# Linear attention taken as (q·k)·v instead of q·(k·v), with whole heads for GpSimd and inverse deviations by exp and ln

## The reference

```python
xn = _ln(q_x, ln1_w, ln1_b)
q, k, v = (heads of xn @ wq + bq, xn @ wk + bk, xn @ wv + bv)   # 16 heads of 16
fq = jax.nn.elu(q) + 1.0
fk = jax.nn.elu(k) + 1.0
kv = jnp.einsum('bhnd,bhne->bnde', fk, v)      # summed over the heads of a token
qkv = jnp.einsum('bhnd,bnde->bhne', fq, kv)
k_sum = fk.sum(axis=1)
qk = jnp.einsum('bhnd,bnd->bhn', fq, k_sum)
attn = qkv / (qk[..., None] + 1e-06)
x = q_x + attn @ wo + bo
x = x + gelu(_ln(x, ln2_w, ln2_b) @ fc_w + fc_b) @ proj_w + proj_b
```

## Time and profile before

| what | value |
|---|---|
| median of 3 runs | 1926.57 us (1924.77 to 1927.19) |
| the profiled execution, its own time | 1925.68 us |
| its span in the profile | 1924.0 us |
| PE, DVE, ACT, POOL busy | 1741.5, 1277.6, 806.8, 1269.4 us |
| mean granted clock of PE | 0.931 |
| chain that ended last | PE 83%, POOL 5%, ACT 5%, DVE 3% |

### The profile page before, as it was taken

The page is one execution under the profiler, slowest core; times in us unless marked ns, Lnnn a source line. Parts: engine busy times, 40 slices in busy tenths (PEclk is TensorE's granted clock), DMA queues, the critical chain, the costliest instruction groups (busy, mean ns, idle before and its releaser), DMA issues.

```text
span 1924.0 us, 26018 instructions
## 1 busy us (share of the span) xinstructions
PE 1741.5 (91%) x7160; PEld 1248.5 (65%) x7161; DVE 1277.6 (66%) x2339; ACT 806.8 (42%) x1547; POOL 1269.4 (66%) x749
## 2 busy tenths in 40 slices
PE   3489998898999989989999899887999999999997
PEld 1255565555655655556556555555888888888886
DVE  7988898988988989889889898713222222222221
ACT  2245455464454554644545546332332333333232
POOL 5876888888988888789888888812333333333333
PEclk8698898998988988989889889888999999999999
DMA  5101110101101101011011010005766666666664
GB/s 187 41 14 44 45 44 22 44 30 36 34 20 44 44 22 44 31 35 44 11 44 44 22 44 24 27 28 171 163 159 157 157 161 162 162 164 159 157 156 91
DMA packets 87130, 148.57 MB, mean 77 GB/s; under 512 B 8640, under 2 KB 71872, under 8 KB 86720
## 3 DMA queue, kind: packets, MB, share of 16 engines
q1 hardware_dynamic: 60512, 112.58, 18.3%
q0 software_dynamic: 26592, 35.67, 11.0%
HBM read 101.79 MB, written 48.56 MB: 78 GB/s over the span
## 4 chain that ended last, share of the span: by engine, by line
PE 83%; POOL 5%; ACT 5%; DVE 3%; issue 2%; DMA 1%; SPq 0%; POOLq 0%; ACTq 0%; DVEq 0%
PE p_b L1210 17%; PE p_b L1258 11%; PE p_b L1289 10%; PE p_b L1350 9%; PE p_b L1361 9%; PE p_q L1350 7%; PE p_q L1182 5%; PE p_v L1350 3%; PE p_b L1281 3%; PE p_v L1182 3%; PE p_b L1196 2%; POOL prod_pool L461 2%; PE p_xT L1337 2%; ACT bT L628 1%; ACT L639 1%
## 5 line engine op out<-in xcount | busy, mean ns | idle before, releaser
L574 POOL DMA_INDIRECT out_rows<-prod_pool,prod x142 | 220.7, 1554 | 384.3 <-ACT prod_pool L742 353.9
L461 POOL TENSOR_TENSOR prod_pool<-prod_pool 128x544 f32<-128x544 f32 (+4 forms) x240 | 399.6, 1665 | 18.8
L1258 PE MATMUL p_b<-bT,fc_sb 128*128 128x512 f32 x512 | 226.5, 601 | 12.1 <-ACT bT L671 12.1
L1210 PE MATMUL p_b<-proj_sb,hid 128*128 128x256 f32 x1024 | 230.5, 379 | 0.0
L834 DVE TENSOR_REDUCE kvT<-prod 128x128 f32<-128x2048 f32 x96 | 219.4, 2286 | 2.7
L826 DVE TENSOR_TENSOR prod<-p_q,v_dve 128x4096 f32<-128x4096 f32 x48 | 211.9, 4414 | 0.0
L1289 PE MATMUL p_b<-bT,sgup_sb 128*128 128x512 f32 x384 | 208.1, 700 | 0.0
L1210 PEld LDWEIGHTS p_b<-proj_sb,hid 128*128 128x128 f32 x1024 | 189.6, 190 | 27.7 <-issue 0.5
L1350 PE MATMUL p_b<-prod,exp_up 128*128 128x256 f32 x840 | 187.1, 379 | 0.0
L1258 PEld LDWEIGHTS p_b<-bT,fc_sb 128*128 128x128 f32 x512 | 96.8, 192 | 132.4 <-issue 108.6
L864 DVE TENSOR_REDUCE qkv<-prod 128x204 f32<-128x3264 f32 x48 | 170.4, 3550 | 3.0 <-DVE rs_a L795 2.3
(11 more groups left out here) (169 smaller groups left out, 2904.0 us busy)
## 6 DMA issues: line engine op xcount, KB each, us to landing
exp_up<-in_experts SPq DMA_DIRECT2D x71, 768.0 KB
prod<-rows_sorted SPq DMA_DIRECT2D x71, 260.0 KB, 2.7
xin<-in_x SPq DMA_DIRECT2D x16, 512.0 KB, 3.3
xres<-in_x SPq DMA_DIRECT2D x16, 512.0 KB, 3.3
out_rows<-x SPq DMA_DIRECT2D x16, 512.0 KB, 3.0
exp_dn<-in_experts SPq DMA_DIRECT2D x8, 384.0 KB, 5.1
out_rows<-prod_pool,prod POOLq DMA_INDIRECT x142, 3.8
rows_sorted<-rows SPq DMA_DIRECT2D x2, 1040.0 KB, 6.5
```

What stands on the lines that cost most here:

```text
L461: done(g.tensor_tensor(prod_pool[:, at:at + n * w], prod_pool[:, at:at + n * w], prod_pool[:, at + n * w:at + 2 * n * w], ALU.add))
L574: pool.indirect_dma_start(out=out[:, :], out_offset=bass.IndirectOffsetOnAxis(ap=tok_i[j][:, a:a + 1], axis=0), in_=yg[j][:, a * D:(a + 1) ...
L1210: ins = t_.matmul(o, src[:, k, t * P:(t + 1) * P], w[:, k, :], start=k == 0, stop=bias_at is None and k == chunks - 1)
L1258: ins = t_.matmul(bnk[:], fc_sb[:, k, f * P:(f + 1) * P], bT[:, k, :], start=k == 0, stop=k == KC - 1)
```

## The change

The order of the two products of the attention is turned: first scores s = fq x fk for every pair of heads (16 x 16 sums of 16), then s x v; the denominator is the sum of a row of scores, so the ones column and the key sum go. The products are 4096 and 4096 for a tile instead of 4096 and 3264 (DVE's 12 heads) or 4352 twice (POOL). POOL keeps tile 0 and takes 8 whole heads of tile 2 (`SPLIT`) instead of 4 heads of the second product of tiles 1, 2 and 3. Keys stand features by heads in `eqk`, where `features` writes them; the scores overwrite q and k in PSUM (`p_qk`). The division of tiles 1 and 2 comes after the features of the next tile, and `release` raises `pq_free`. `residual_2` is split: all first sums of tile 3 stand between its halves, and behind it the totals. On ACT the square root becomes Ln, then Exp with a factor -0.5, from one table set that is loaded explicitly at three places of a round; the reciprocals on DVE go. ACT takes q, k, v of the next tile 0 after LN3's rows instead of before LN3's square root. The first choice is cast into PSUM and copied from there to `rows`; a small sum of `weights` is kept in PSUM. `weights` comes before the last `pq_free`. POOL's scores of tile 0 stand at the head of its round before the shared gate, the halving waits for `attn_ready`.

```diff
-DVE_HEADS = 12
-POOL_HEADS = HEADS - DVE_HEADS
+SPLIT = 2
+POOL_HEADS = 8
...
-            def heads(c, u):
-                wait(pool, share_ready, 3 * c + u)
...
-                announce(pool, halve(qkv[u % 2][:, DVE_HEADS:, :].rearrange("p h e -> p (h e)"), at),
-                         share_done, 3 * c + u)
+            def scores(q, k, n):
+                return g.tensor_tensor(
+                    prod_pool[:, 0:n * HH].rearrange("p (d h g) -> p d h g", d=HD, g=HEADS),
+                    q.rearrange("p (h d) -> p d h", d=HD).unsqueeze(3).to_broadcast([P, HD, n, HEADS]),
+                    k.rearrange("p (d g) -> p d g", d=HD).unsqueeze(2).to_broadcast([P, HD, n, HEADS]), ALU.mult)
+            def mixed(sc, v, n):
+                return g.tensor_tensor(
+                    prod_pool[:, 0:n * HH].rearrange("p (g h e) -> p g h e", g=HEADS, e=HD),
+                    sc.rearrange("p h g -> p g h").unsqueeze(3).to_broadcast([P, HEADS, n, HD]),
+                    v.unsqueeze(2).to_broadcast([P, HEADS, n, HD]), ALU.mult)
+            def heads(c):
+                wait(pool, feat_ready, 4 * c + SPLIT + 1)
+                own = slice(HEADS, HEADS + POOL_HEADS)
+                features = eqk[SPLIT % 2]
+                announce(pool, scores(features[:, (HEADS - POOL_HEADS) * HD:D], features[:, D:2 * D], POOL_HEADS),
+                         share_qk_used, c + 1)
+                announce(pool, halve(flat(s_pool[:, own, :])), pool_s, c + 1)
+                announce(pool, mixed(s_pool[:, own, :], v_dve[SPLIT % 2][:].rearrange("p e g -> p g e"),
+                                     POOL_HEADS), share_v_used, c + 1)
+                done(halve(flat(qkv_pool[:, own, :])))
             def body(c, core, stage_b, tail):
+                if core:
+                    wait(pool, feat_ready, 4 * c + 1)
+                    announce(pool, scores(fqk_pool[:, 0:D], fqk_pool[:, D:2 * D], HEADS), pool_qk_used, c + 1)
                 if tail and (core or stage_b):
                     gate_shared(c)
                 if core:
...
+                    wait(pool, attn_ready, c)
+                    done(halve(flat(s_pool[:, 0:HEADS, :])))
...
                 if core:
...
+                    heads(c)
+                    announce(pool, mixed(s_pool[:, 0:HEADS, :], v_pool[:], HEADS), pool_v_used, c + 1)
+                    announce(pool, halve(flat(qkv_pool[:, 0:HEADS, :])), pool_qkv, c + 1)
...
+            def rsqrt(out, var, log, std, n):
+                a.activation(var, var, ACT.Ln).then_inc(log, 1)
+                act.wait_ge(log, n)
+                a.activation(out, var, ACT.Exp, scale=-0.5).then_inc(std, 1)
+            def table_exp_ln():
+                a.preload_act_table_set("natural_log_exp_and_others")
...
-                done(v.reciprocal(rs_b[:, 0], sq_b[:]))
+            def products_1(u):
+                n = own_heads(u)
+                done.later(v.tensor_tensor(
+                    prod[:, 0:n * HH].rearrange("p (h d g) -> p h d g", h=n, g=HEADS),
+                    p_qk[u % 2][:, 0:n * HD].rearrange("p (h d) -> p h d", h=n).unsqueeze(3)
+                    .to_broadcast([P, n, HD, HEADS]),
+                    eqk[u % 2][:, D:2 * D].rearrange("p (d g) -> p d g", d=HD).unsqueeze(1)
+                    .to_broadcast([P, n, HD, HEADS]), ALU.mult))
+            def sums_1(u, lo, hi):
+                done.later(v.tensor_reduce(
+                    p_qk[u % 2][:, lo * HEADS:hi * HEADS].rearrange("p (h g) -> p h g", g=HEADS),
+                    prod[:, lo * HH:hi * HH].rearrange("p (h d g) -> p h g d", d=HD, g=HEADS), AX.X, ALU.add))
-                done.later(v.tensor_copy(rows[:, :, C_E0], top_i[:, :, 0]))
                 done(v.tensor_copy(first2, top_i[:, :, 0:2].rearrange("p t s -> p s t")))
+                done.later(v.tensor_copy(rows[:, :, C_E0], first2[:, 0, :]))
...
-                    features(c, 3)
-                    kv_products(3)
-                if stage_b:
-                    residual_2(c)
-                    scales_b(ln3_std, ln3_scale, c)
+                    features(c, 3)
...
+                    products_1(3)
+                if stage_b:
+                    residual_2(c, 0)
+                if core:
+                    sums_1(3, 0, HEADS)
+                if stage_b:
+                    residual_2(c, 1)
+                if core:
+                    totals(3, total[:, 0:HEADS])
+                    wait(dve, pool_s, c + 1)
+                    done.later(v.tensor_reduce(total[:, HEADS:], s_pool[:], AX.X, ALU.add))
+                if stage_b:
+                    scales_b(ln3_std, ln3_scale, c)
```

More of the change, by code:

```diff
@@ L201, in build @@
         neg_top = tail[:, 0:TPB]
+        gap_1 = tail[:, 80:80 + TPB]
         first2 = tail[:, 32:32 + 2 * TPB].rearrange("p (s t) -> p s t", s=2)
@@ L654, in body @@
                     norm(lambda t: xmid[:, t, :], lambda t: xres[:, t, :], a_scale, a_ready)
+                table_exp_ln()
                 if core:
-                    table(ACT.Exp, 3)
                     take_qkv(c, 2)
                 if stage_b:
-                    table(ACT.Sqrt)
                     wait(act, ln2_var, c)
-                    a.activation(sq_b[:], sq_b[:], ACT.Sqrt).then_inc(ln2_std, 1)
+                    rsqrt(rs_b[:, 0, :], sq_b[:], ln2_log, ln2_std, c)
                     wait(act, ln2_scale, c)
@@ L666, in body @@
                     wait(act, ln1_var, c + 2)
-                    a.activation(sq_a[:], sq_a[:], ACT.Sqrt).then_inc(ln1_std, 1)
+                    rsqrt(rs_a[:, 0:2], sq_a[:], ln1_log, ln1_std, c + 2)
                 if stage_b:
@@ L685, in body @@
                     take_x(c + 1, 1)
-                    take_qkv(c + 1, 0)
                 if stage_b:
-                    table(ACT.Sqrt)
                     wait(act, x1_read, c)
-                    a.activation(sq_b[:], sq_b[:], ACT.Sqrt).then_inc(ln3_std, 1)
+                    rsqrt(rs_b[:, 0, :], sq_b[:], ln3_log, ln3_std, c)
                     wait(act, ln3_scale, c)
@@ L708, in _ @@
             act.wait_ge(tmp_ready, 1)
+            table_exp_ln()
             wait(act, ln1_var, 1)
-            a.activation(sq_a[:], sq_a[:], ACT.Sqrt).then_inc(ln1_std, 1)
+            rsqrt(rs_a[:, 0:2], sq_a[:], ln1_log, ln1_std, 1)
             norm_1(0)
@@ L793, in ln1_scales @@
                 wait(dve, ln1_std, b + 1)
-                done(v.reciprocal(rs_a[:, 0:2], sq_a[:]))
                 v.scalar_tensor_tensor(rs_a[:, 2:4], mv_a[:, :, 0].unsqueeze(1).to_broadcast([P, 2, TPB]), -1.0,
@@ new lines, in features, with own_heads @@
+                if u == 0:
+                    feature(fqk_pool, 0, 2 * D).then_inc(feat_ready, 1)
+                else:
+                    own = own_heads(u) * HD
+                    done.later(feature(e, D, 2 * D))
+                    if own < D:
+                        done.later(feature(e, own, D))
+                    feature(y, 0, own).then_inc(feat_ready, 1)
+                    dve.wait_ge(feat_ready, n + 1)
+            def own_heads(u):
+                return HEADS - POOL_HEADS if u == SPLIT else HEADS
@@ L968, in weights @@
                 wait(dve, gap_exp, c)
-                done(v.tensor_scalar(gap[:], gap_e[:], 1.0, None, ALU.add))
-                done(v.reciprocal(rows[:, :, C_W0], gap[:]))
+                done(v.tensor_scalar(gap_1, gap_e[:], 1.0, None, ALU.add))
+                done(v.reciprocal(rows[:, :, C_W0], gap_1))
                 v.tensor_tensor(rows[:, :, C_W1], gap_e[:], rows[:, :, C_W0], ALU.mult).then_inc(slots_ready, 1)
@@ L993, in body @@
                         ln1_stats(c + 1)
-                    kv_sums_2(c, 1)
-                    q_products(c, 1, last)
+                    sums_1(1, half, HEADS)
+                    totals(1, den_1[:, 0:HEADS])
+                    products_2(c, 1, False)
                     if not last:
                         ln1_scales(c + 1)
+                    guard(den_1[:, 0:HEADS])
+                    sums_2(1)
+                    inverse(den_1[:, 0:HEADS])
+                    if not last:
                         dve.wait_ge(ln1_scale, c + 2)
-                        dve.sem_inc(pq_free, 1)
-                    q_sums(1)
+                    wait(dve, attnT_psum, KC * c)
                     features(c, 2)
-                    kv_products(2)
+                    done.sync()
+                    done.later(divide(0, 0, qkv[1][:], den_1[:, 0:HEADS]))
+                    release(c, 1)
+                    products_1(2)
                 if tail:
```

218 lines of the change are left out of this document (97 added, 121 removed).

## The result

The changed kernel takes 1971.89 us (median of 4 runs, 1970.37 to 1972.11) against 1925.7 before: the ratio is 1.0237, with a 95% interval of 1.022 to 1.0255. It is slower by 46 us where 35 us less were forecast, and outside the range. The profiled execution took 1972.11 us, its span is 1970.4, the mean granted clock 0.921 (before 0.931).

A forecast was written before the change was run, and what follows sets the result against it. Waits were taken to bound it: PE idles for LN3, which hangs on DVE's chain. 14 x 1.65 + 6 + 4 gave 33 to 35 us off 1925.7, so about 1891 us, range 1848 to 1922.

The forecast's parts named there:

- two prices that the trace doesn't show directly: Costs of first sums reading products 64 bytes apart and of scores written back to PSUM; both taken as none.
- the path: DVE's chain from the attention's residual to LN3's last statistic, forecast to shrink from 45.9 to 44.3 us.
- Rival 1: Strided first sums on DVE cost 1.5 times, 4.3 us more before LN3; about 1948 us; chance 11%.
- the ends: First and last rounds, where DVE waits openly for POOL: savings of 6 and 4 us.
- its neighbours: POOL or an unforeseen table load as new wait in LN3's tail, 1935 to 1950 us; 15% with Rival 1.
- The table load's end: ACT's 1283 ns table load leaves DVE's wait before LN3; with a second activation added, 1.2 us saved.
- The round of 75.1: Forecast time of a middle round: 76.8 less 1.65 us, with the low clock costing what it costs now.
- PE's gap: TensorE's idle wait for the normalized rows after LN3, forecast to fall from 3.79 to 2.2 us.
- The 4 us that DVE saves are nearly all saved outside this path: DVE's smaller work per round falls behind LN3; ahead of it 33.4 us are lost and 33.5 gained.
- Scores back to PSUM: Writing DVE's scores over q and k in PSUM: no cost, or at most 0.1 us each.
- Rival 2: TensorE's clock stays up in its light stretch, rounds near 72 us, total 1850 us; chance 15%.
- Rival 3: DVE's chain to LN3 is 1 us longer than summed; no gain per round, 1915 us; chance 16%.

The follow-up runs named there:

- keys by heads: Changed kernel with key columns laid out heads by features, so DVE's first products and sums run over neighbours and POOL reads keys across: 1895.12 us, ratio 0.9843.
- the first weight in PSUM: Kernel of keys by heads with the first routing weight made in PSUM and copied to `rows`, so L990 reads one SBUF operand: 1891.63 us, ratio 0.9822.

## Why the prediction was wrong

**The step that failed** is the first of the "two prices that the trace doesn't show directly": "At 1.5 times the time per element the first would show 33 ns more. So I take no cost". The row it rests on the earlier trace rows is a sum of pairs, and pairs are free at a step of 128 bytes (2.29 us for 2048) where sums of four and of sixteen cost 3.57. The inference from 64 elements in pairs to 4096 in sixteens carried the whole sum: 8192 elements a round on the path, 5.4 us. The rule of the Trainium skill (SBUF — State Buffer, Door 1: The DMA port swizzle), that each access which crosses to a new line of 16 bytes pays, was weighed and set aside for this row; the first sums of 3.67 and 7.11 us bear it out. It has no size for the penalty, and pairs 128 bytes apart, which it doesn't except, take no longer than neighbours here (2.29 us).

**Rival 1 was the mechanism**, a strided sum on the path to LN3, with the price too small: 1.5 was an upper bound without a row under it, measured are 1.60 and 1.61. It gave a path of 48.6, a gap of 6.4 and rounds of 78.5 to 79.5; measured are 49.55, 7.22 and 80.22. It took the sums at 8.5 us, where the path above it has them at 9.0, and 2.2 us a round, the middle of its span, where its own path gives 2.6. It also let the ends give 10 us back. At the first transposes (145.20 against 144.84 before) nothing is left of that, since the sums lie on the way of the first rounds too, and the last two rounds lose 2.4. So 1948 became 1972. Its 11%, 15 with its neighbours, was too little for a price bounded by one row of 64 elements.

**The other steps stand**, as keys by heads show, where only the failed price is gone (POOL's scores apart):

- The path was summed as 44.3; it is 43.9 there. The table load's end was put at 1.2 us; the wait went from 1.90 to 0.41 and 0.60, and is 1.88 again with the square root.
- The round of 75.1 is 75.15, in part by luck. PE's gap is 2.80 and not 2.2, with DVE late behind L990; and the first matmuls of the shared expert take 6.90, where before they take 8.19 and 7.06 in turn, 7.6 on average, and not 8.19 in each round. 0.6 more and 0.7 less cancel. With L990 out of the way the gap is 1.80 and the matmuls take 7.93, and again the round is 75.1: that the slow stretch costs what it cost before was not borne out, only the sum of the two was.
- The first transposes come at 139.17 against 144.84, 5.7 us earlier (forecast 6). The 13 rounds to the transposes at 1114.03 (1143.71 before) give 24.0, the rest 3.8 (forecast 4). The profiled execution took 1892.21 against 1925.7, 33.5 us less, where the sum said 33 to 35.
- "The 4 us that DVE saves are nearly all saved outside this path": over eight middle rounds DVE is busy 517.1 us with the first weight in PSUM, against 550.3 before, 4.1 less a round; and a further 4.42 us taken from behind the path are worth 1.1 us in all, which is within the spread.
- POOL: the scores of 16 heads take 7.54 us (L478), the crossed product of 2048 takes 4.87, forecast 7.55 and near 4.8. No wait of DVE for POOL is left in the middle rounds; POOL waits instead, 10 us for ACT ahead of the shared gate in the round of 80.80 that starts at 706.38, and 1.5 us there with keys by heads.
- Scores back to PSUM cost nothing: sums over neighbours written there take 2.29 us, as those of the earlier trace rows written to SBUF.
- Rival 2, the clock staying up, didn't come about: even at a gap of 0.81 the clock falls, only later, and the mean granted clock from 503.14 to 946.16 is 0.96 (before, in the middle rounds, 0.92). Rival 3 fell too, since the path was summed right.

## What to carry to other kernels

Look at the innermost axis of every DVE operand before the operations are counted: a step of 16 bytes or more between fp32 elements cost 1.5 to 1.7 times here, for reads and writes, sums and products alike, pairs apart, and a rearranged layout moves the price unless all users agree with it. When a price is inferred from a small row, its pattern must be the same down to the length of the inner axis; where it isn't, keep the bound in the sum. And price work by whether it stands ahead of what the critical engine waits for: 4.42 us a round were worth 18 us in all on one side of LN3 and nothing clear of the spread on the other.

## What the runs showed of the hardware that was not expected

- **Steps on DVE.** 2048 fp32 in groups of 16: 2.29 us at steps of 4 and 8 bytes, 3.74, 3.81, 3.57 and 3.58 at 16, 32, 64 and 128. Pairs at 128 bytes take 2.29 as well, fours at 64 bytes 3.57.
- **A DVE product with both operands in SBUF waited for the end of POOL's.** 2.89 us for 4 elements, ending with POOL's product of 9.54 us; 0.15 with one operand in PSUM, with POOL at work all through. The wait was there in all 14 rounds in which two SBUF operands met POOL's product. Whether it takes a POOL product that reads across, as this one did, no run shows. The Trainium skill (GPSIMD Engine Reference, 8. Key points) names contention of the two engines for DVE instructions with two SBUF inputs; here it was the whole rest of POOL's instruction.
- **Reading across on POOL** made the scores of 4096 take 9.54 us in place of 7.54, 27% more, and those of 2048 4.87 in place of 3.87. The Trainium skill (GPSIMD Engine Reference, 7. Performance pitfalls for Q7 kernels) has about half more per element for kernels that read at steps over 8 bytes; the trace shows less.
- **A shorter wait need not shorten the round.** With PE's wait 1.00 us shorter the twelve matmuls behind it took 1.03 us longer (6.90 to 7.93) at the lower clock, and the round stayed 75.1. Where the clock falls near an idle piece, read the wait and the slow stretch behind it as one.
